# Graph attention with residual norm: the last pair's output by column halves in V's block order, the last row's statistics on VectorE, one power for two rows

## What is computed

```python
output = einsum('bni,io->bno', x, weight)
q = einsum('bni,io->bno', x, wq)
k = einsum('bni,io->bno', x, wk)
alpha = einsum('bno,bmo->bnm', q, k)
alpha = maximum(alpha, 0.0) * (adj != 0)
alpha = softmax(alpha, axis=1)
x = _layernorm(x + einsum('bnm,bmo->bno', alpha, output), axis=-1)
```

## Time and profile before

| what | value |
|---|---|
| median of three runs | 530.29 us |
| the profiled execution, its own time | 531.49 us |
| its span, first to last instruction | 529.7 us |
| mean granted TensorE clock | 0.999 of full speed |
| TensorE matmul busy | 520.2 us, 98% |
| weight load busy | 496.8 us, 94% |
| VectorE busy | 387.6 us, 73% |
| ScalarE busy | 328.9 us, 62% |
| GpSimd busy | 285.7 us, 54% |
| HBM traffic | 45.09 MB read, 16.78 MB written |

### The profile page before, as it was taken

One profiled execution on the slowest core, in us unless ns is written; L12 is line 12 of the kernel. 1 busy time (PEld: TensorE's weight loads), 2 busy tenths in 40 slices (PEclk: granted clock), 3 DMA queues, 4 the chain that ended last, 5 costly groups with the idle time before them and its releaser, 6 DMA issues.

```text
span 529.7 us, 10990 instructions
## 1 busy us (share of the span) xinstructions
PE 520.2 (98%) x3823; PEld 496.8 (94%) x3823; DVE 387.6 (73%) x724; ACT 328.9 (62%) x780; POOL 285.7 (54%) x212
## 2 busy tenths in 40 slices
PE   7999999999999999999999999999999999999995
PEld 5889999999999999999999999999999999999993
DVE  4766969497785958779496776949777695877657
ACT  5565485575657566665665666557575756766464
POOL 0387847384572838547283654728457373854002
PEclk9999999999999999999999999999999999999999
DMA  7504361522506133160523407052250614304022
GB/s 266 210 0 172 109 236 43 188 92 80 200 0 213 66 138 139 54 223 0 198 79 118 159 10 260 8 198 79 84 193 0 222 55 159 119 0 160 1 80 79
DMA packets 24243, 62.12 MB, mean 117 GB/s; under 512 B 1312, under 2 KB 2336, under 8 KB 22304
## 3 DMA queue, kind: packets, MB, share of 16 engines
q1 hardware_dynamic: 24224, 61.87, 32.7%
HBM read 45.09 MB, written 16.78 MB: 117 GB/s over the span
## 4 chain that ended last, share of the span: by engine, by line
PE 97%; DVE 1%; DMA 1%; issue 0%; POOLq 0%; POOL 0%; SPq 0%; ACT 0%; ACTq 0%
PE o_bank L238 12%; PE o_bank L239 12%; PE o_bank L240 12%; PE chain L238 11%; PE chain L240 11%; PE chain L239 11%; PE bank_y L238 6%; PE bank_y L240 6%; PE bank_y L239 6%; PE bank_z L240 3%; PE bank_z L238 3%; PE bank_z L239 3%; DMA xn<-in_w 1%; PE chain L369 0%; PE chain L375 0%; PE chain L374 0%
## 5 line engine op out<-in xcount | busy, mean ns | idle before, releaser
L960 POOL TENSOR_TENSOR s_lo<-xs,s_hi 128x512 fp32r<-128x512 f32 x60 | 89.5, 1520 | 101.3 <-ACT s_hi L495 101.3
L502 ACT COPY parts<-chain 128x256 f32<-128x256 f32 x180 | 66.9, 372 | 92.4 <-PE chain L240 91.1
L954 POOL TENSOR_TENSOR a_lo<-xt,a_hi 128x512 fp32r<-128x512 f32 x60 | 79.9, 1357 | 48.3 <-ACT a_hi L488 48.3
L240 PE MATMUL o_bank<-t_hi,a_lo 128*128 128x256 f32 x256 | 72.4, 283 | 0.0
L239 PE MATMUL o_bank<-t_lo,a_hi 128*128 128x256 f32 x256 | 72.4, 283 | 0.0
L238 PE MATMUL o_bank<-t_hi,a_hi 128*128 128x256 f32 x256 | 72.4, 283 | 0.0
L555 ACT ACTIVATE squares<-xn,neg_mean 128x512 f32<-128x512 f32 x64 | 46.3, 723 | 30.6 <-DVE neg_mean L756 26.0
L741 DVE SCALAR_TENSOR_TENSOR p_lo<-soft,inv_sum,p_hi 128x256 fp32r<-128x256 f32 x64 | 59.6, 948 | 3.0 <-ACT p_hi L545 3.0
L688 DVE TENSOR_TENSOR v_lo<-parts,v_hi 128x512 fp32r<-128x512 f32 x45 | 59.8, 1354 | 2.6 <-ACT v_hi L535 2.6
L524 ACT CAST t_hi<-parts 128x512 fp32r<-128x512 f32 x45 | 27.9, 621 | 47.0 <-DVE parts L703 38.9
L749 DVE SCALAR_TENSOR_TENSOR xn<-o_bank,xn 128x512 f32<-128x512 f32 x64 | 44.1, 690 | 10.5 <-PE o_bank L240 10.0
(11 more groups left out here) (171 smaller groups left out, 1727.7 us busy)
## 6 DMA issues: line engine op xcount, KB each, us to landing
xn<-in_x SPq DMA_DIRECT2D x16, 1024.0 KB, 5.2
xt<-in_x_t SPq DMA_DIRECT2D x15, 1024.0 KB, 4.8
out<-xn SPq DMA_DIRECT2D x15, 1024.0 KB, 4.2
adj<-in_adj_t SPq DMA_DIRECT2D x16, 512.0 KB, 3.4
xt<-in_x_t SPq DMA_DIRECT2D x4, 256.0 KB, 4.5
xn<-in_w SPq DMA_DIRECT2D x4, 256.0 KB, 4.7
xn<-in_wq_t SPq DMA_DIRECT2D x4, 256.0 KB, 5.9
parts<-in_wk_t SPq DMA_DIRECT2D x4, 256.0 KB, 5.9
```

The source lines that it names most:

```text
L240: return nc.tensor.matmul(dst, a[1], b[0], start=False, stop=last, skip_group_check=shared)
L502: nc.scalar.copy(dst[:, c], src[:, c]).then_inc(copied, 1)
L954: nc.gpsimd.tensor_tensor(a_lo[:, slot, a], xt[:, a], a_hi[:, slot, a].bitcast(F32), ALU.subtract).then_inc(a_lo_ready, 1)
L960: nc.gpsimd.tensor_tensor(s_lo[:, s], xs[:, s], s_hi[:, s].bitcast(F32), ALU.subtract).then_inc(s_lo_ready, 1)
```

## The change

1. TensorE: the last pair's O is made by `fill_last_o`, by blocks of V in the order A11, A22, A12, A21. Each block gives one half of the columns of two rows: 12 matmuls of 256 columns. Rows 0 and 1 are complete in the third block, rows 2 and 3 in the fourth. The right half of row 3 goes into `bank_z` and is announced by a semaphore of its own.
2. ScalarE and VectorE: all four splits of p stand ahead of V's blocks, and the blocks come in the order A22, A11, A12, A21.
3. VectorE: row 3's right half is added to x ahead of row 0, its left half behind row 2; each half gets a BN_STATS, the two are joined by a BN_AGGR, which gives mean and variance with no use of ScalarE.
4. GpSimd: rows 0 and 1 keep their own power, rows 2 and 3 share one on two columns, which waits for both variances.
5. Normalising: rows 0, 1 and 3 on VectorE, all behind the last variance; row 2 on ScalarE, in two passes, by the centred row in `squares`.
6. SyncE: the stores' order is rows 0, 1, 3, 2.

```diff
+V_LAST = {A22: 1, A11: 2, A12: 3, A21: 4}
...
+        last_row_half = bank_z[:, 1]
...
-            for r in range(R):
-                sp.wait_ge(normed, R * (PAIRS - 1) + r + 1)
+            for r in (0, 1, R - 1, R - 2):
+                if r == R - 2:
+                    sp.wait_ge(scaled, 1)
+                else:
+                    sp.wait_ge(normed, R * (PAIRS - 1) + min(r, 2) + 1)
                 sp.dma_start(out_rows[PAIRS - 1][:, r], xn[:, 1, r]).then_inc(y_stored[1], 16)
...
+            def fill_last_o():
+
+                p = PAIRS - 1
+                for u in (A11, A22, A12, A21):
+                    g, j = u // 2, u % 2
+                    pe.wait_ge(p_lo_ready, R * p + M * g + M)
+                    pe.wait_ge(v_lo_ready, R * p + V_LAST[u])
+                    for n in range(M):
+                        rows = slice(n * P, (n + 1) * P)
+                        for m in range(M):
+                            t = g * M + m
+                            last = add_chunk(last_row_half if (u, n) == (A22, M - 1) else o_bank[g * M + n][:, j],
+                                             (p_hi[:, t, rows], p_lo[:, t, rows]),
+                                             (v_hi[:, t, j], v_lo[:, t, j]), m == 0, m == M - 1, True)
+                        if u in (A12, A21):
+                            last.then_inc(o_filled, 1)
+                        elif (u, n) == (A22, M - 1):
+                            last.then_inc(half_filled, 1)
...
-            fill_o(PAIRS - 1, last=True)
+            fill_last_o()
...
                     split_p(p, 1)
+                    split_p(p, 2)
+                    split_p(p, 3)
...
+                    split_v(p, A22)
+                    split_v(p, A11)
                     split_v(p, A12)
-                    split_v(p, A11)
-                    split_p(p, 2)
-                    split_v(p, A22)
-                    split_p(p, 3)
                     split_v(p, A21)
...
-            for r in range(R):
+            for r in range(R - 1):
                 centred_squares(PAIRS - 1, 1, r, by_tile=True)
+            r = R - 2
+            act.wait_ge(squared, R * PAIRS - 1)
+            nc.scalar.activation(squares[:], xn[:, 1, r], ACT.Identity, bias=neg_mean[:, r:r + 1]).then_inc(centred, 1)
+            act.wait_ge(rstd_ready, PAIRS + R - 2)
+            act.wait_ge(centred, 1)
+            nc.scalar.activation(xn[:, 1, r], squares[:], ACT.Copy, scale=rstd[:, r:r + 1]).then_inc(scaled, 1)
...
+            def last_half(j, first):
+
+                row, cols = xn[:, 1, R - 1], slice(j * N, (j + 1) * N)
+                if first:
+                    dve.wait_ge(half_filled, 1)
+                else:
+                    dve.wait_ge(o_filled, R * PAIRS)
+                nc.vector.tensor_tensor(row[:, cols], last_row_half if j else o_bank[R - 1][:, 0], row[:, cols], ALU.add).then_inc(half_added, 1)
+                dve.wait_ge(half_added, 1 if first else 2)
+                nc.vector.bn_stats(half_stats[:, j], row[:, cols]).then_inc(half_measured, 1)
+
+            last = PAIRS - 1
+            dve.wait_ge(xn_loaded[1], 16 * (PAIRS // 2))
+            last_half(1, True)
+            for r in range(R - 1):
+                residual(last, 1, PAIRS // 2 - 1, r)
                 mean_of(r)
                 if r >= 1:
                     variance_of(r - 1)
-                if r >= 2:
-                    normalise_last(r - 2)
-            variance_of(R - 1)
-            normalise_last(R - 2)
-            normalise_last(R - 1)
+            last_half(0, False)
+            dve.wait_ge(half_measured, 2)
+            nc.vector.bn_aggr(row_stats[:], half_stats[:]).then_inc(row_aggregated, 1)
+            dve.wait_ge(row_aggregated, 1)
+            nc.vector.tensor_scalar(var_eps[:, R - 1:R], row_stats[:, 1:2], EPS, None, ALU.add).then_inc(last_var_ready, 1)
+            variance_of(R - 2)
+            for r in range(R - 2):
+                normalise_last(r)
+
+            dve.wait_ge(rstd_ready, PAIRS + R - 2)
+            nc.vector.tensor_scalar(xn[:, 1, R - 1], xn[:, 1, R - 1], row_stats[:, 0:1], rstd[:, R - 1:R],
+                                    ALU.subtract, ALU.mult).then_inc(normed, 1)
...
-            for r in range(R):
+            for r in range(R - 2):
...
+            pool.wait_ge(last_var_ready, 1)
+            pool.wait_ge(var_ready, PAIRS + R - 2)
+            nc.gpsimd.tensor_tensor(rstd[:, R - 2:R], var_eps[:, R - 2:R], minus_half[:, R - 2:R],
+                                    ALU.pow).then_inc(rstd_ready, 1)
```

More of the change, by code:

```diff
@@ L99, in gnn_resnorm @@
         minus_half = sb("minus_half", [P, R])
+        half_stats = sb("half_stats", [P, 2, 6])
+        row_stats = sb("row_stats", [P, 2])
         c1, c2, c3, c22, c11, c21 = (parts[:, i] for i in range(6))
@@ L156, in gnn_resnorm @@
         v0_filled, v_hi_ready, v_lo_ready = sem("v0_filled"), sem("v_hi_ready"), sem("v_lo_ready")
-        s_filled, o_filled = sem("s_filled"), sem("o_filled")
+        s_filled, o_filled, half_filled = sem("s_filled"), sem("o_filled"), sem("half_filled")
         masked, max_ready, exp_ready = sem("masked"), sem("max_ready"), sem("exp_ready")
         inv_ready, p_hi_ready, p_lo_ready = sem("inv_ready"), sem("p_hi_ready"), sem("p_lo_ready")
+        half_added, half_measured, row_aggregated = sem("half_added"), sem("half_measured"), sem("row_aggregated")
+        last_var_ready, centred, scaled = sem("last_var_ready"), sem("centred"), sem("scaled")
         added, mean_ready, squared = sem("added"), sem("mean_ready"), sem("squared")
@@ L438, in fill_s, with fill_o @@
                     last.then_inc(s_filled, 1)
-            def fill_o(p, first=False, last=False):
+            def fill_o(p, first=False):
                 for g in range(2):
@@ L445, in fill_o @@
                     else:
-                        pe.wait_ge(v_lo_ready, R * p + (2 if last and g == 0 else 3 + g))
+                        pe.wait_ge(v_lo_ready, R * p + 3 + g)
                     for n in range(M):
@@ L706, in _ @@
             T_AT, V_AT = {A22: 1, A11: 2, A12: 3, A21: 4}, {A22: 1, A12: 2, A11: 3, A21: 4}
-            V_LAST = {A12: 1, A11: 2, A22: 3, A21: 4}
             def split_t(p, u):
@@ L809, in step @@
                 else:
-                    split_p(p, 0)
-                    split_p(p, 1)
+                    for r in range(R):
+                        split_p(p, r)
+                    split_v(p, A22, V_LAST)
+                    split_v(p, A11, V_LAST)
                     split_v(p, A12, V_LAST)
-                    split_v(p, A11, V_LAST)
                     sum_c21(m)
-                    split_p(p, 2)
-                    split_v(p, A22, V_LAST)
-                    split_p(p, 3)
                     split_v(p, A21, V_LAST)
@@ L924, in normalise_last @@
                                         ALU.add, ALU.mult).then_inc(normed, 1)
-            for r in range(R):
-                residual(PAIRS - 1, 1, PAIRS // 2 - 1, r)
+            def last_half(j, first):
[12 more added lines that the diff above has]
+                residual(last, 1, PAIRS // 2 - 1, r)
                 mean_of(r)
```

## The result

The changed kernel took 532.88 us (median of 8 runs, 532.01 to 534.86) beside 530.40 for the kernel before (8 runs, 530.21 to 532.24). The ratio is 1.0046, 95% interval 1.0027 to 1.0065. In a later comparison (11 runs against 33 shared ones) it was 533.09 against 531.26, ratio 1.0033, interval 1.0022 to 1.0044. The forecast was 532.2, range 531.2 to 532.9, slower.

The account below looks back on a forecast made before the run. TensorE's matmuls (98% of the span) bound the kernel, then a closing chain. Last fill +0.74, VectorE late +0.64, add to last issue +0.38, stores +0.31: +2.07, less 0.15, taken as +1.9 on 530.29: 532.2 us, range 531.2 to 532.9.

Parts of the forecast that it names:

- VectorE late: VectorE's closing queue: row 3's left half, filled at 524.54, is added only at 525.22, 0.64 us late.
- the queue of stores: Closing stores: landings can't be closer than 0.67 us, so the last lands at 531.30, not 530.99: +0.31.
- Order of p and V: VectorE's splits ahead of V's blocks: second block ready at 518.38, O starts at 518.53, +0.42 us.
- Halves: O on TensorE: 48 matmuls of 256 columns at 0.12 take 5.76 us against 5.44 for 24, +0.32.
- Statistics: Row 3's halves on VectorE: BN_STATS taken as 0.42 us (bounds 0.27 to 0.84), BN_AGGR 0.18 (upper 0.4).
- Power held until behind the second normalising: GpSimd's shared power: held by VectorE's normalisings, it ends 0.40 + 0.16 behind the second, at 528.04; run free, 527.34.
- From the left half's add to the last issue: Closing chain, 525.22 to 528.99: 3.77 us against 3.39 from row 3's add before, +0.38.
- Stores overlap: Rival on the closing stores: last landing 2.0 behind its issue, at 530.99; +1.76 less 0.15, 531.9; chance 0.10.
- The power runs free: Rival on GpSimd's shared power: ends at 527.34, last store issued at 528.33; +1.81 less 0.15, 531.95; chance 0.14.
- VectorE keeps its pitch: Rival, row 0's add to row 2's variance: under 3.0 us, not 3.9; left half about 524.6; 531.3 us; chance 0.10.
- Statistics are dear: Rival on VectorE's statistics: BN_STATS 0.84, BN_AGGR 0.4; up to 533.2 us, 532.7 if half true; chance 0.15.
- the change doesn't shift O at all: Rival on O's matmuls: fills come no later, the shorter closing part wins; needs 48 under 5.1 us; faster, chance 0.03.

Follow-up runs that it names:

- the two powers of one column above: Against the kernel before: O starts with V's first block, row 3 added ahead of all normalising, single powers; 530.01 us against 531.05, ratio 0.9987, tail 16.69.

## Why the prediction was right, and where its terms were off

The time in the tail: forecast +1.9, measured +1.87. Step by step, on the old clock (the changed profile less 0.92):

| step | forecast | measured |
|---|---|---|
| O's first matmul | 518.53 | 518.52 |
| O's last fill | 524.54 | 524.51 |
| row 0's add | 522.49 | 522.54 |
| row 3's left half added | 525.22 | 525.27 |
| power done | 528.04 | 527.65 |
| row 3 normalised | 528.61 | 528.23 |
| last store issued | 528.99 | 528.63 |

By the terms of the sum: last fill +0.74, measured +0.71; VectorE late +0.64, measured +0.72 (0.76 behind the fill, where before it was 0.04); from that add to the last issue +0.38, measured -0.03; the queue of stores +0.31, measured +0.47. The terms add up to +2.07 and the measured ones to +1.87, so the forecast's total is right to 0.2, while its last two terms are well off, in opposite directions.

*Order of p and V, +0.42.* Right: 518.52, and +0.42 when done alone.

*Halves, +0.32, and VectorE late, +0.64.* Right in size and in mechanism. The fill of row 3 is 0.71 later than the 523.80 of before, and the left half's add starts 0.76 behind that fill. The runs with parts of the change separate them: 17.02, +0.42 for the order of p, +0.89 for halves (and V's blocks in the new order) with rows 0 and 1 complete after 24 matmuls, +0.52 for completing them after 36, +0.04 for the new closing part: 18.89. Of the 0.89, 0.29 is the later fill and 0.60 is row 3's add waiting for VectorE. The matmul time of the Trainium skill's page "VectorE: DVE Perf Modes", section "The TRN2 errata", by which I estimated 0.109 us for a half, against which I took the rows' 0.12, would have put the fill half a microsecond too early.

*Statistics.* BN_STATS 0.43 for my 0.42, BN_AGGR 0.21 for 0.18. I had then taken 0.15 off the sum because the lower bound seemed nearer. That was wrong, and only by luck did it cover most of the 0.2 by which the terms were too high.

*Power held until behind the second normalising, done at 528.04.* This step failed: the term was too large, and with it fell one of my signs, a power of over 1.2 us. I had put in 1.41 and it took 0.87. It was done at 527.65: in the changed profile's own time it started at 527.70, behind the first normalising's start (527.47) and ahead of the second's (527.93), and ended 0.56 behind the end of the first. That is 0.40 + 0.16 as in my rule, but of the first, not the second, and the two powers of one column above show that the rule isn't general. Nor was the second slowed by the power that was already running: the two took 0.99 together, 0.54 each with their usual overlap. The Trainium skill, page "SBUF — State Buffer", section "Who interferes with whom", says of VectorE's two-port modes, which it says `tensor_scalar` can enter, that whoever issues first gets the shared pair for its whole instruction and the other fully blocks. That a power behind a normalising is held agrees with this trace (0.87 against 0.70), the one of 0.54 above doesn't. That the second one, in its turn, waits for a power isn't seen here: by the page the second normalising would have waited.

*From the left half's add to the last issue, 3.77.* Measured 3.36 (526.19 to 529.55), 0.39 of the difference being the power. So this stretch is as long as the one before (3.39), and my +0.38 for it is zero. What the chain gained without the square, row 2's store took back: row 3's own store is issued 2.99 behind the add (529.18), and row 2's another 0.37 behind it.

*Stores, +0.31.* Right in kind, too small: 0.47. The last store took 2.4 to land instead of 2.0, and the data ran without a gap. My sum let row 3's store land 2.0 behind its issue and so gave the two early stores no part in the delay; the run with two small stores shows that they have 0.18 of it.

*Rivals.* "Stores overlap" falls with that run. "The power runs free" would be 0.17 better than what happened, nearer to the truth than my held case. "VectorE keeps its pitch" falls: the left half was added at 525.27, not 524.6. "Statistics are dear" falls, and so does "the change doesn't shift O at all": the 48 matmuls took 6.0 us. The first comparison's median stands 0.6 further above before than the tail does, in the later one the two agree (1.83 and 1.87). So that excess is scatter of the start-up, for which I had no term; the range's upper end, 532.9, was just enough for it, by luck.

## What to carry to other kernels

When the last product of a kernel is cut so that its parts start in the order of their inputs, look at when each consumer's row is *complete*: two rows that finish together at the end give the next engine a queue where it had gaps, and that costs more than the finer cut can bring. A cut pays where it lets the first piece start earlier (one block of V instead of two, with the splits left as they were), and work that has slack, here the normalising of early rows, belongs behind the add on the critical chain (0.17 us here). Putting that work at the very end has a price of its own: it meets the last power, and the early rows' stores then queue up with the last ones.

For differences of 0.3% in a kernel whose start-up scatters by as much, measure from a fixed event just ahead of the edit to the end: it repeated to 0.01 us where medians moved by one.

## What the runs showed of the hardware that I had not expected

A power on GpSimd that started 0.16 to 0.17 us behind a single normalising's start on VectorE took 0.77 to 0.79 us with one column, and 0.55 with none beside it; for two columns, beside two normalisings, it was 0.87 against 0.70. One that started 0.08 behind a normalising's start took 0.54. A row's add from PSUM didn't hold it: in the changed kernel the power at 525.45 took 0.55 beside the add at 525.28. And a second normalising issued while a power ran kept its 0.54.

BN_STATS over 256 float32 columns in SBUF takes 0.43 us and BN_AGGR over two of its results 0.21. For one row in two halves that is 1.07 on VectorE, more than the 0.85 from the start of ScalarE's square over 512 columns to the variance.
